# A one-core RWKV-6 and feed-forward kernel: a feed-forward piece, a mix and a scaling change places, and GpSimd makes two of eight diagonal copies

## What is computed

```python
x_prev = pad(x)[:, :t]; xx = x_prev - x
mix = tanh((x + xx * time_maa_x) @ maa_w1).reshape(b, t, 5, 32)
mw, mk, mv, mr, mg = einsum('btfe,fec->fbtc', mix, maa_w2)
xw, xk, xv, xr, xg = (x + xx * (time_maa_i + m_i) for each of the five)
r, k, v, g = xr @ Wr.T, xk @ Wk.T, xv @ Wv.T, silu(xg @ Wg.T)
decay = exp(-exp(time_decay + tanh(xw @ td_w1) @ td_w2))
# per head, 32 keys and 32 values, over time:
y_t = r_t (S + u * k_t v_t);  S = decay_t * S + k_t v_t
y = group_norm(y) * ln_g + ln_b
x = layernorm(x + (y * g) @ Wo.T)
h = gelu(x @ ternary(W_fc).T)                # 512 -> 2048
x = layernorm(x + layernorm_affine(h) @ ternary(W_proj).T)
```

## Time and profile before

| what | value |
|---|---|
| median of 3 runs | 3530.97 us (3509.68, 3530.97, 3533.42) |
| the profiled execution | 3509.35 us, its span 3507.2 us |
| granted TensorE clock over the span | 0.983 of full |
| busy: PE, DVE, ACT, POOL | 90%, 71%, 54%, 22% |
| HBM traffic | 49.97 MB read, 16.78 MB written, 19 GB/s |
| chain that ended last, by engine | PE 25%, DVE 22%, issue 21%, ACT 19%, POOL 10% |

### The profile page before, as it was taken

One profiled execution on the slowest core, in us unless ns is written; L12 is line 12 of the kernel. 1 busy time (PEld: TensorE's weight loads), 2 busy tenths in 40 slices (PEclk: granted clock), 3 DMA queues, 4 the chain that ended last, 5 costly groups with the idle time before them and its releaser, 6 DMA issues.

```text
span 3507.2 us, 98753 instructions
## 1 busy us (share of the span) xinstructions
PE 3143.1 (90%) x39261; PEld 2257.9 (64%) x39261; DVE 2473.1 (71%) x5108; ACT 1897.2 (54%) x3852; POOL 784.9 (22%) x725
## 2 busy tenths in 40 slices
PE   1899999999999999999999999999999999999997
PEld 0566666766666766666666666766666766666764
DVE  8466686776676676776766776676786776677776
ACT  0445556645566555566555566555566655556653
POOL 3122211122221122221222221222211122221121
PEclk9899999999999999999999999999999999999998
DMA  4000000000000000000000000000000000000000
GB/s 184 14 8 19 20 14 17 17 14 20 14 17 20 17 14 20 14 17 20 17 14 20 14 17 20 17 14 20 14 19 18 17 20 14 20 14 17 20 17 13
DMA packets 22598, 73.04 MB, mean 21 GB/s; under 512 B 3041, under 2 KB 3297, under 8 KB 20545
## 3 DMA queue, kind: packets, MB, share of 16 engines
q1 hardware_dynamic: 22208, 66.76, 5.4%
HBM read 49.97 MB, written 16.78 MB: 19 GB/s over the span
## 4 chain that ended last, share of the span: by engine, by line
PE 25%; DVE 22%; issue 21%; ACT 19%; POOL 10%; POOLq 1%; DMA 1%; ACTq 1%; DVEq 0%; SPq 0%
PE psP L393 7%; ACT ARENA L653 7%; PE psP L423 6%; ACT HHI L810 6%; POOL MT L856 5%; POOL ARENA L870 4%; PE psF L615 4%; ACT GG L801 3%; DVE ARENA L1125 3%; DVE ARENA L1087 3%; DVE ARENA L1077 2%; DVE HLO L1237 2%; DVE SUMS L1229 2%; DVE GR L1245 2%; PE psX L375 1%
## 5 line engine op out<-in xcount | busy, mean ns | idle before, releaser
L393 PE MATMUL psP<-ARENA,WALL 128*128 128x256 f32 x3072 | 692.0, 382 | 0.2 <-ACT ARENA L684 0.2
L653 ACT ACTIVATE ARENA<-ARENA 32x512 f32<-32x512 f32 (+1 forms) x992 | 578.8, 583 | 189.8 <-DVE ARENA L1077 137.7
L393 PEld LDWEIGHTS psP<-ARENA,WALL 128*128 128x128 f32 x3072 | 574.6, 190 | 84.5 <-issue 11.3
L1237 DVE SCALAR_TENSOR_TENSOR HLO<-GG,FWB,HHI 128x128 f16<-128x128 f32 x1024 | 292.3, 347 | 459.8 <-ACT HHI L810 455.7
L615 PE MATMUL psF<-XHI,WFC 128*128 128x128 f16 x4096 | 490.0, 220 | 46.5 <-DVE XLO L1216 34.0
L615 PE MATMUL psF<-XLO,WFC 128*128 128x128 f16 x4096 | 488.8, 220 | 0.0
L615 PEld LDWEIGHTS psF<-XHI,WFC 128*128 128x128 f16 x4096 | 401.7, 99 | 88.1 <-issue 86.0
L615 PEld LDWEIGHTS psF<-XLO,WFC 128*128 128x128 f16 x4096 | 402.9, 98 | 14.0 <-issue 10.3
L870 POOL TENSOR_TENSOR ARENA<-ARENA,XT 128x1024 f32<-128x1024 f32 x128 | 285.2, 2228 | 507.4 <-DVE ARENA L1029 507.4
L634 PE MATMUL psF<-WPJ,HHI 128*128 128x512 f16 x1024 | 389.8, 381 | 3.1 <-ACT GG L801 3.1
L634 PE MATMUL psF<-WPJ,HLO 128*128 128x512 f16 x1024 | 388.1, 379 | 0.0
(11 more groups left out here) (166 smaller groups left out, 5418.0 us busy)
## 6 DMA issues: line engine op xcount, KB each, us to landing
XT<-x_ch SPq DMA_DIRECT2D x33, 520.0 KB, 3.4
ARENA<-x_tok SPq DMA_DIRECT2D x32, 512.0 KB, 4.1
out<-OUT SPq DMA_DIRECT2D x64, 256.0 KB, 2.0
WALL<-w_all SPq DMA_DIRECT2D x5, 1024.0 KB, 16.6
ARENA<-wfc SPq DMA_DIRECT2D x4, 1024.0 KB, 7.9
ARENA<-wpj SPq DMA_DIRECT2D x3, 1024.0 KB, 14.6
GG<-wpj SPq DMA_DIRECT2D x1, 1024.0 KB, 18.6
OUT<-w2a SPq DMA_DIRECT2D x8, 64.0 KB, 14.9
```

The costliest lines, as they stand in the source:

```text
L393: mm = pe.matmul(psP[:, P.bank(f"{name}{g}"), COLS * c:COLS * (c + 1)], WALL[:, w, k, 128 * (2 * g + c):128 * (2 * g + c + 1)], cc(XF[slot ...
L653: return act.activation(o, i, ACT.Copy)
L1237: e = dve.scalar_tensor_tensor(out=HLO[:, k, :], in0=GG[:, u % 2, 0, 128 * m:128 * (m + 1)], scalar=FWB[:, 0, k:k + 1], in1=HHI[:, k, :], ...
```

## The change

- **TensorE.** mix mw stands between the two halves of `wo`. down(1,3) moves into the next body, behind `td1`.
- **DVE, end of the body.** up(1,3), the reduction for stats(1) (now in two halves, L1298 in the changed file) and `stored` move from in front of the gating (or just behind) to behind it. `decay_input` moves between the two X1 additions.
- **The buffers XF swap roles**: decay's mix goes to XF[1], so that it may be written while `wo` still reads XF[0].
- **DVE, start of the body.** `late` falls into four parts: moments behind mix mk, product behind mix mv, normed and stored around up(0,0). GpSimd's roots move with them.
- **Ring F** has a table of banks: up(0,0) now follows stats(1) in its bank and up(1,0) follows stats(0), where both followed the product.
- **Levels.** level 2's right scaling stands in front of up(0,3) on DVE; ACT's second half of the gate moves one level on; the reduction for stats(0) is cut in two, behind levels 4 and 8.
- **Diagonal copies.** For p = 1, ACT makes two of four; GpSimd makes the others as a product with ones, counted by `ab_rest`.

```diff
+F_BANKS = [0, 1, 0, 1, 0, 1, 1, 0, 1, 0, 1, 0]
...
-        i = self.names.index(name) - self.depth
+        own = self.names.index(name)
+        i = next(i for i in range(own - 1, own - 1 - self.n, -1) if self.banks[i % self.n] == self.banks[own])
...
-        F = Ring(F_SEQ, 2, f_full, {"act": f_act, "stats": f_stats, "product": f_product})
+        F = Ring(F_SEQ, 2, f_full, {"act": f_act, "stats": f_stats, "product": f_product}, banks=F_BANKS)
...
                 mm.then_inc(p_full, 1)
+                if ffn:
+                    ffn.late()
...
                     mm.then_inc(p_full, 1)
+                    if p == 0:
+                        mix(it, 0, "mw", wait_free)
                 if ffn:
                     ffn.stats(1)
-                mix(it, 0, "mw", wait_free)
-                if ffn:
-                    ffn.down(1, 3)
...
+                def late():
+                    if not first:
+                        down(before, 1, 3)
...
+                    if i == 0 and ffn:
+                        ffn.up(0, 3)
+                    if i == 1:
                         gate(1)
...
-                    for q in range(4):
+                    for q in range(2 if p else 4):
...
-                    v = XF[f % 2].rearrange("p (q t) -> p q t", t=CH)
+                    v = XF[(f + 1) % 2].rearrange("p (q t) -> p q t", t=CH)
                     pool.tensor_tensor(v, v, xcur, ALU.add).then_inc(xf_ready, 1)
-                    if f == 2 and ffn:
+                    if f == 1 and ffn:
                         ffn.late()
...
+                        if ffn:
+                            ffn.late_normed()
...
+                pool.wait_ge(k1_odd, it + 1)
+                if ffn:
+                    ffn.settled()
+                pool.wait_ge(y_full, 2 * it + 1)
+                pool.wait_ge(w_dve, W.read(it, "l16"))
+                for q in range(2, 4):
+                    if q == 3:
+                        pool.wait_ge(ab_rest, 2 * it + 1)
+                    r = slice(BLK * q, BLK * (q + 1))
+                    block = A[r, 512:1024].rearrange("p (h t) -> p h t", h=HEADS)
+                    pool.tensor_tensor(AB[r, :, BLK * q:BLK * (q + 1)], block, ONES[r, 0:BLK].unsqueeze(1).broadcast_to([BLK, HEADS, BLK]), ALU.mult).then_inc(ab_rest, 1)
+                pool.wait_ge(ab_rest, 2 * it + 2)
...
+                mix(t, 0, "mw", None)
                 dve.wait_ge(m_dve, M.read(t, "mw1"))
-                v = XF[0].rearrange("p (q t) -> p q t", t=CH)
+                v = XF[1].rearrange("p (q t) -> p q t", t=CH)
                 dve.tensor_tensor(v, v, xcur, ALU.add).then_inc(xf_ready, 1)
...
                 if ffn:
+                    ffn.moments()
                     ffn.normalise()
@@ -1059,3 +1095,5 @@
                 if ffn:
+                    ffn.late_normed()
                     ffn.up(0, 0)
+                    ffn.late_stored()
...
                     ffn.up(0, 2)
+                scale_right(1, 2)
+                if ffn:
                     ffn.up(0, 3)
                 for i, n in enumerate(LEVELS):
-                    scale(i + 1, n)
+                    if i:
+                        scale_right(i + 1, n)
+                    scale_left(i + 1, n)
...
-                scale(5, 32, ffn.fold if ffn else None)
+                    if ffn and n in (4, 8):
+                        ffn.fold(0, n // 4 - 1)
+                scale(5, 32)
...
-                if ffn:
-                    ffn.up(1, 3)
-                    ffn.stored()
...
                 if ffn:
-                    ffn.stats(1)
+                    ffn.up(1, 3)
+                    ffn.fold(1, 0)
+                    ffn.fold(1, 1)
+                    ffn.stored()
 
@@ -1195,3 +1247,4 @@
                     dve.bn_stats(BNS[:, p, :], X1[:, p, :]).then_inc(bn_done, 1)
-                decay_input(it, "wo1")
+                    if p == 0:
+                        decay_input(it)
...
+                    dve.tensor_reduce(GR[:, i, :], SUMS[:, i, :].rearrange("p (m t) -> p t m", m=4), AX.X, ALU.add).then_inc(sums_folded, 1)
...
+                def moments(j, p):
 
@@ -1254,9 +1311,12 @@
                     dve.wait_ge(st_step, s + 1)
+                    dve.tensor_scalar(st[:, 3:4], st[:, 0:1], st[:, 2:3], st[:, 1:2], ALU.mult, ALU.add).then_inc(st_step, 1)
+                    dve.wait_ge(st_step, s + 2)
+                    dve.tensor_scalar(FV[:, p:p + 1], st[:, 3:4], 0.0, LN_EPS, ALU.max, ALU.add).then_inc(st_step, 1)
 
+                def product(j, p):
+
+                    st, s = ST[:, p, :], 4 * (PAIRS * j + p)
+                    dve.wait_ge(f_full, F.full(j, f"pj_{p}"))
                     pj = psF[:, F.bank(f"pj_{p}"), :]
                     dve.scalar_tensor_tensor(out=pj, in0=WSUM[:, :], scalar=st[:, 2:3], in1=pj, op0=ALU.mult, op1=ALU.add)
-                    dve.scalar_tensor_tensor(out=st[:, 3:4], in0=st[:, 0:1], scalar=st[:, 2:3], in1=st[:, 1:2],
-                                             op0=ALU.mult, op1=ALU.add).then_inc(st_step, 1)
-                    dve.wait_ge(st_step, s + 2)
-                    dve.tensor_scalar(FV[:, p:p + 1], st[:, 3:4], 0.0, LN_EPS, ALU.max, ALU.add).then_inc(st_step, 1)
```

89 lines of the change are left out of this document (53 added, 36 removed).

## The result

| what | before | changed |
|---|---|---|
| median | 3531.43 us (3509.68 to 3533.42) | 3343.78 us (3343.21 to 3345.63) |
| ratio, with its 95% interval | | 0.9479 (0.9447 to 0.9512) |
| the profiled execution, its span | 3509.35, 3507.2 us | 3343.92, 3342.1 us |
| granted TensorE clock over the span | 0.983 | 0.993 |

A forecast was written before the change was run, and what follows sets the result against it. TensorE's work plus its idle time bounds the kernel. Six steps sum to -2.86 us in each of 31 bodies, -88.7; with clock falls -25.6 and +22, 3509.35 becomes 3417 us; stated range 3340 to 3500, forecast's own 3380 to 3465.

The forecast's parts named there:

- a rival that had 0.17: No collision behind the gate: GpSimd's pieces give way, diagonal copies in time, no clock loss; 3334 us, chance 0.17.
- D: Delay of up(1,3) on DVE from GpSimd's mix_low running beside it behind the gate: 1.6 us, bounds 0 and 2.65.
- td1's wait: Sign in the profile after: TensorE waits for decay's sum at td1, between 1 and 2.5 us.
- step 6: From the gate to channels k: -1.15 us from the new order, plus a 1.6 us collision delay, +0.45 a tile.
- the falls of the clock that didn't come: TensorE's clock falling in front of td1, as often as in the profiled execution: 15 x 1.5 = +22 us.
- 1. gate: Output projection: with up(1,3) and stored behind the gating, the gated output comes 1.8 us sooner; -1.75 us a tile.
- 2. XLO: In front of up(0,0): only the product of the late end still precedes XLO, so its wait goes; -1.13 us a tile.
- 3. diagonal copies: Second chunk product: splitting copies between ACT and GpSimd cuts the 0.88 wait to 0.35; -0.5 us, bounds -0.88 and 0.
- 4. spread roots: ACT enters up(1,0) 1.28 us sooner, so the chain to the roots ends about 0.35 sooner; -0.35 us a tile.
- 5. levels: Levels: earlier scaling helps levels 4 and 8, reduction halves delay 16 and 32; +0.42 us, bounds -2.3 and +1.2.
- Whole exclusion: Rival: up(1,3) and mix_low exclude each other for whole instructions, copies gain nothing, clock falls in 30 tiles; 3494 us, chance 0.16.
- slow GpSimd copies: Rival: GpSimd's diagonal copies become the wait; 3510 us at 2.7 us a copy, 3591 at 4.0; chance 0.15.

The follow-up runs named there:

- the kernel that had the wait: Changed kernel with ACT's rounded copy of the first four tanh blocks made ahead of the second tanh, so mix_low starts with up(1,3): 3419.59 us.

## Why the prediction was right, and where its numbers were not

The forecast was "faster", and that holds. The number was saved by its range: the time is below the 3380 to 3465 that the forecast gave itself, and near the 3334 of a rival that had 0.17. Three of the prediction's own signs came out against it: up(1,3) isn't longer by D, td1's wait is not between 1 and 2.5 us (2.1 us in 7 waits), and the second of GpSimd's copies took 2.13 and not at most 1.6. Of the 73 us between 3417 and the result, step 6 has 44, the falls of the clock that didn't come 22 and the ends of the program 14; the copies take 15 back, and the other steps give the rest.

Per tile in us, measured by stage in the two traces:

| step | forecast | measured |
|---|---|---|
| 1. gate | -1.75 | -1.79 |
| 2. XLO | -1.13 | -1.13 |
| (OUT in front of up(0,0), 0.15 in before, left out) | 0 | -0.15 |
| 3. diagonal copies | -0.5 | -0.03 |
| 4. spread roots | -0.35 | -0.45 |
| 5. levels | +0.42 | +0.48 |
| 6. gate to channels k | +0.45 | -0.98 |
| sum | -2.86 | -4.05 |

**Steps 1, 2, 4 and 5** hold. The gate's wait is 0.09, XLO has none, level 8 waits 0.90 (forecast 0.9), levels 16 and 32 wait 1.05 and 0.94, stats(0) not at all. The sizes come out because each was a difference of two starts in one stretch of the trace.

**Step 6** failed in one term, D, of 1.6. Its sentence was that GpSimd "runs `mix_low` beside them: eight pieces with 0.08 between, from 0.24 after the gate". The 0.24 was read where the gate came last. But step 1 had just brought the gate 1.8 us forward, and then ACT's rounded copy came last, 0.8 later. I asked of VectorE and TensorE what is late next, and not of GpSimd. Started together, the two do cost 1.59 us, one piece let through in front of each small instruction, as the text had it; only the big sum paid nothing, where 0.4 was booked. So the size is right for a meeting that the changed kernel doesn't have, and in part by luck: 1.6 was the middle of two readings, 0.9 and 2.0. The same step's 17.4 is 17.33 by its own rows, which changes nothing. In its place the changed kernel pays 0.52 at mix mw, for the late and once blocked pieces, and 0.26 on average at mix mk, for the turn of TensorE's loop. Against the kernel with up(1,3) put back, the two and what goes with them cost 0.9; without that the step would be about -1.9, an estimate.

The Trainium skill, "SBUF — State Buffer", section "SBUF: two separate sides", has the loser of the pair wait for the whole instruction of the other. In the traces the loser ends 0.15 us behind the winner's piece, though it takes 0.35 alone, so a part of it runs within the other's time. The 2.65 that the prediction took for D by this rule was five meetings of 0.53; there were three, and each did cost 0.53. What the rule gets right is that at each meeting of `mix_low` with up(1,3) one of the two keeps its ordinary time. It gives the pair to the one that starts first, and the recorded starts don't bear that out: in the changed kernel the piece started 0.07 to 0.08 us ahead of the sum in all 30 bodies, and it was the piece that paid.

**Step 3**: the term was taken at half of the wait and brought 0.03 at the copies, for the reason given as its bound: the difference for XX blocked the second copy (2.13 for 1.27). Taken with step 4 the two came to -0.48 for a forecast of -0.85; what the copies didn't bring, part of it went to the roots.

**The clock.** The loss at the projection went, 25.6 us, as forecast. The new falls in front of td1, +22, didn't come, because the wait there didn't. In the kernel that had the wait they came, 17 in 29 tiles at 1.4 for a forecast of 15 at 1.5.

**What no step had**: 14 us outside the bodies' stages, at the ends of the program. 10.0 of them are the last feed-forward part, which stands alone behind the last L1164 (77.6 us, now 67.6). There the new table of banks lets up(0,0) and up(1,0) start behind the moments and no longer behind the product. That shows in two waits, which give 2.8 and 2.95 of the 10.0; what gives the rest of it, and the other 4, stays open. Their first rows on PE, before and after:

```profile
3456.67 0.27 PE L615 MATMUL psF<-XHI,WFC 128*128 128x128 f16 x1 [4.52 <-DVE OUT L1266]
...
3479.34 0.26 PE L615 MATMUL psF<-XHI,WFC 128*128 128x128 f16 x1 [3.29 <-DVE OUT L1266]
```

```profile
3295.23 0.26 PE L623 MATMUL psF<-XHI,WFC 128*128 128x128 f16 x1 [1.72 <-DVE ST L1308]
...
3316.97 0.22 PE L623 MATMUL psF<-XHI,WFC 128*128 128x128 f16 x1 [0.34 <-DVE ST L1308]
```

Together: 31 x 4.05 = 125.6, 25.7 of clock and 14 make 165.4, which is 3509.35 - 3343.92.

**The rivals.** The one with no collision came nearest, and for the wrong half of its reasons: GpSimd's pieces gave way to the sum only, and the copies were not in time. Whole exclusion and slow GpSimd copies are out: neither D of 2.65 nor a copy of 2.7 us was seen.
